# A four-layer graph network on one core: first pass by slots with four x buffers, halved adjacency loads, later weight loads, shorter batch norms, one more layer norm by slots, and a reordered last step

## What is computed

```python
x = LN(x + L0(x, adj))  # A_hat x; W1, batch norm, relu; W2, batch norm
x = LN(x + L1(x, adj))  # edge softmax attention over 256 edges, 4 heads
x = LN(x + L2(x, adj))  # (adj*adj) mixes before W1 (128->256), W2 (256->512), W3 (512->128)
x = LN(x + L3(x, adj))  # dense masked attention
```

## Time and profile before

| | |
|---|---|
| three runs | 565.99, 568.5, 569.31 us; median 568.5 |
| the profiled execution's own time | 569.67 us |
| its span, first to last instruction | 567.8 us |
| granted TensorE clock, mean | 0.987 of full speed |
| TensorE matmul busy | 533.0 us, 94% of the span |
| VectorE, ScalarE, GpSimd busy | 419.2, 373.9, 198.8 us |

### The profile page before, as it was taken

How to read it: one execution, slowest core, us unless ns; L and a number is a source line. 1 busy time by engine, 2 the same in 40 slices (tenths; PEclk the granted TensorE clock), 3 DMA queues, 4 the chain that set the end, 5 groups by cost and what they waited for, 6 DMA issues and landing times.

```text
span 567.8 us, 11229 instructions
## 1 busy us (share of the span) xinstructions
PE 533.0 (94%) x3522; PEld 464.6 (82%) x3522; DVE 419.2 (74%) x1466; ACT 373.9 (66%) x749; POOL 198.8 (35%) x240
## 2 busy tenths in 40 slices
PE   7899999797999989999999999999999999999871
PEld 5788734575887988998999999999998998989861
DVE  4588677889787644479787787788688776778887
ACT  4577594676656636256695785786787687685681
POOL 7930350337366312315226126216216116210203
PEclk9899999999999999999999999999999999999997
DMA  8222100132100000000000100100100100100012
GB/s 227 76 81 74 39 0 0 55 95 64 48 0 2 1 0 1 1 2 1 1 2 2 37 1 0 38 0 0 37 0 0 37 0 0 39 0 2 1 38 74
DMA packets 28383, 15.26 MB, mean 27 GB/s; under 512 B 2320, under 2 KB 28048, under 8 KB 28352
## 3 DMA queue, kind: packets, MB, share of 16 engines
q1 hardware_dynamic: 27792, 13.65, 8.4%
q0 software_dynamic: 560, 1.25, 0.7%
HBM read 10.69 MB, written 4.19 MB: 26 GB/s over the span
## 4 chain that ended last, share of the span: by engine, by line
PE 76%; DVE 13%; ACT 3%; issue 2%; POOL 2%; DMA 1%; SPq 1%; DVEq 0%; POOLq 0%; ACTq 0%
PE psum L291 14%; PE psum L293 14%; PE psum L292 14%; PE psum L2004 9%; PE psum L1811 5%; PE psum L1859 3%; PE psum L1946 3%; PE psum L1956 3%; PE psum L1883 2%; PE psum L1870 2%; PE psum L1874 2%; PE psum L2050 2%; PE psum L2032 2%; DVE ln_st L188 2%; DVE soft L1029 1%
## 5 line engine op out<-in xcount | busy, mean ns | idle before, releaser
L207 POOL TENSOR_TENSOR ln_r<-ln_v,mhalf 128x8 f32<-128x8 f32 x27 | 44.6, 1651 | 225.7 <-DVE ln_v L201 225.7
L2004 PE MATMUL psum<-l2w_s,h 128*128 128x128 f32 x512 | 59.8, 276 | 0.0
L2004 PEld LDWEIGHTS psum<-l2w_s,h 128*128 128x128 f32 x512 | 59.0, 192 | 0.8
L291 PE MATMUL psum<-qt_hi,l2w_s_hi 128*128 128x512 f32 x128 | 52.8, 412 | 0.0
L293 PE MATMUL psum<-qt_hi,l2w_s_lo 128*128 128x512 f32 x128 | 50.8, 396 | 0.0
L292 PE MATMUL psum<-qt_lo,l2w_s_hi 128*128 128x512 f32 x128 | 50.7, 396 | 0.0
L285 ACT ACTIVATE keep_x<-keep_x,ln_b,ln_r (+1 forms) x108 | 44.4, 487 | 8.2 <-DVE keep_x L277 5.6
L1559 ACT ACTIVATE h<-psum 128x512 f32<-128x512 f32 x60 | 34.8, 593 | 11.7 <-PE psum L293 11.6
L291 PE MATMUL psum<-wgt_hi,h_hi 128*128 128x256 f32 x128 | 37.1, 290 | 0.9 <-DVE h_lo L1006 0.9
L293 PE MATMUL psum<-wgt_hi,h_lo 128*128 128x256 f32 x128 | 35.8, 280 | 0.0
L292 PE MATMUL psum<-wgt_lo,h_hi 128*128 128x256 f32 x128 | 35.8, 279 | 0.0
(11 more groups left out here) (284 smaller groups left out, 1746.8 us busy)
## 6 DMA issues: line engine op xcount, KB each, us to landing
xin<-in_x SPq DMA_DIRECT2D x64, 128.0 KB, 2.3
out_x<-ob SPq DMA_DIRECT2D x24, 128.0 KB, 1.8
out_x<-keep_x SPq DMA_DIRECT2D x8, 128.0 KB, 1.9
l2w_raw<-in_l2w POOLq DMA_DIRECT2D x1, 512.0 KB, 5.8
adjs<-in_adj SPq DMA_DIRECT2D x1, 256.0 KB, 2.8
adjs<-in_adj_t SPq DMA_DIRECT2D x1, 256.0 KB, 3.0
l2w_s<-in_l2w POOLq DMA_DIRECT2D x1, 256.0 KB, 5.5
w_raw<-in_w_t SPq DMA_DIRECT2D x1, 128.0 KB, 3.0
```

Source lines behind the costliest of these rows:

```text
L207: pool.tensor_tensor(ln.r[:].rearrange("p s k -> p (s k)"), ln.v[:].rearrange("p s k -> p (s k)"), mhalf[:], ALU.pow).then_inc(ln.root, 1)
L291: pe.matmul(o, lhs[0], rhs[0], start=start, stop=False)
L2004: i = pe.matmul(bank(s)[:, 0, k * D:(k + 1) * D], h2[:, s, g, j * N + t * P:j * N + (t + 1) * P], l2w3_s[:, g, :], start=(g == 0), stop=(g ...
```

## The change

The diff, cut to its core. What is left out of it declares semaphores and one tile (`off_diag`, ones with a zero diagonal, made on GpSimd by a fill and two selects of 128 x 256), renumbers waits, and adds in the last step: `end_norm_stats(n)` for n of 2 and 3 (the sums of pair 6, statistics from their slots), `end_power` and `sixth_shift` on GpSimd for the same, `fifth_stats` and `fifth_moments` (pair 5's statistics by slots), and `end_exps(s, j)` by halves. On VectorE x0_low, agg_low, h_stats and on ScalarE x0_high, agg_high, h_raw now take one slot each; `last_stats` reads the hidden values from PSUM. For slot 0 the aggregate is made in two banks, and copied and subtracted by halves.

```diff
 def _(sp):
-    sp.dma_start(adj_sb, adj.rearrange("(t p) m -> p t m", p=P)).then_inc(s_adj, 16)
-    sp.dma_start(adjt_sb, adj_t.rearrange("(t p) m -> p t m", p=P)).then_inc(s_adj, 16)
...
-    sp.dma_start(w1_raw[:], w1_t).then_inc(s_small, 16)
+    for t in range(T):
+        sp.dma_start(adj_sb[:, t, :], adj[t * P:(t + 1) * P, :]).then_inc(s_adj[t], 16)
+    def first_load(q, k):
+        for t in range(T):
+            sp.dma_start(xn[:, 4 + k, t, :, :], x_nat[:, t, bass.ds(2 * q, 2), :]).then_inc(x_in[k], 16)
...
+    for k in range(2):
+        first_load(k, k)
+    sp.dma_start(w1_raw[:], w1_t).then_inc(s_first, 16)
+    for k in range(2, 4):
+        first_load(k, k)
+    for k, v in enumerate((src, dst)):
+        sp.dma_start(edge_i[:, k, :], v.partition_broadcast(P)).then_inc(s_edge, 16)
+    sp.dma_start(ecol_i[:].rearrange("p a t -> p (a t)"), edge_cols).then_inc(s_edge, 16)
     sp.dma_start(w2t[:], w2_t.rearrange("(k p) o -> p k o", p=P)).then_inc(s_small, 16)
     sp.dma_start(bnp[:], bn_cols).then_inc(s_small, 16)
     sp.dma_start(l3a_s[:], l3a).then_inc(s_small, 16)
-    for k, v in enumerate((src, dst)):
...
+        for k in range(4):
+            sp.wait_ge(x0_lo, 4 * g + k - 3)
+            first_load(4 * g + k, k)
+    sp.wait_ge(x0_lo, Q)
...
-            sp.wait_ge(x0_lo, 2 * p + s - 1)
...
     i.then_inc(keys_compared, 1)
+    for to, frm in ((wvq[:, 0, :], wv_t), (wvq[:, 1, :], wq_t), (wot[:], wo_t),
+                    (l2w1_raw[:], l2w1), (l2w2_raw[:], l2w2.rearrange("(k p) g -> p k g", p=P)),
+                    (l2w3_s[:], l2w3.rearrange("(k p) g -> p k g", p=P)), (l3w_s[:], l3w), (l3wt_s[:], l3w_t)):
+        pool.dma_start(to, frm).then_inc(s_wts, 16)
     pool.wait_ge(ranks_ready, 1)
...
-    for q in range(4):
-        if q >= 2:
+    for q in range(6):
+        if 2 <= q < 4:
             pool.wait_ge(ln0_done[1], q - 1)
         first_power(pool, q, ln0, q < 2)
-    ln_power(pool, 2, ln0)
-    with pool.Fori(2, IT - 1) as p:
+    for s in range(2):
+        split_x1(2, s, False)
+    ln_power(pool, 3, ln0)
+    with pool.Fori(3, IT - 1) as p:
...
-    dve.tensor_tensor(degc[:, 2, :], degc[:, 0, :], degc[:, 1, :], ALU.subtract).then_inc(deg_ready, 1)
-    dve.wait_ge(at_ready, 1)
+    dve.wait_ge(at_ready, T)
+    dve.tensor_tensor(degc[:, 2, :], degc[:, 0, :], degc[:, 1, :], ALU.add).then_inc(deg_ready, 1)
...
-    link(dve.tensor_copy(a_hat[0][:], at1[:]))
-    dve.tensor_tensor(a_hat[1][:], at1[:], a_hat[0][:], ALU.subtract).then_inc(a_hat_ready, 1)
...
+        dve.scalar_tensor_tensor(out=at1[:, t, :], in0=at1[:, t, :], scalar=dinv[:, t:t + 1],
+                                 in1=bank(0)[:, 0, 0:N], op0=ALU.mult, op1=ALU.mult).then_inc(at_scaled, 1)
+    for t in range(T):
+        dve.wait_ge(a_hat_hi, t + 1)
+        dve.tensor_tensor(a_hat[1][:, t, :], at1[:, t, :], a_hat[0][:, t, :], ALU.subtract).then_inc(a_hat_ready, 1)
+    x0_low(1, 1)
...
+    for s in range(2):
+        agg_low(s, s)
+        x0_low(2 + s, 2 + s)
+    def pass1(p, k):
+        for s in range(2):
+            agg_low(2 * p + s, s)
+            x0_low(2 * p + 2 + s, k + s)
+            h_stats(2 * p - 2 + s)
+    pass1(1, 0)
...
     dve.wait_ge(keys_compared, 1)
     dve.tensor_reduce(rank[:], less[:], AX_X, ALU.add).then_inc(ranks_ready, 1)
-    x0_low(1)
-    with dve.Fori(1, IT - 1) as p:
-        agg_low(p)
-        x0_low(p + 1)
-        h_stats(p - 1)
-    agg_low(IT - 1)
-    h_stats(IT - 2)
-    h_stats(IT - 1)
+    pass1(2, 2)
+    with dve.Fori(1, (IT - 2) // 2) as g:
+        for i in range(2):
+            pass1(2 * g + i + 1, 2 * i)
+    agg_low(Q - 2, 0)
+    h_stats(Q - 4)
+    dve.wait_ge(h_out, Q - 2)
+    dve.bn_stats(bst1[:, 0, Q - 3, :], hraw[:, 0, Q - 3, :])
+    agg_low(Q - 1, 1)
+    dve.bn_stats(bst1[:, 1, Q - 3, :], hraw[:, 1, Q - 3, :]).then_inc(h_stat, 1)
+    for s in range(2):
+        last_stats(Q - 2 + s, s)
     dve.wait_ge(h_stat, Q)
...
-        bn_link(dve.tensor_tensor(shift, shift, scale, ALU.mult))
-        return dve.tensor_tensor(shift, shift, beta, ALU.add)
+        for n, k in enumerate(range(ks.start, ks.stop)):
+            i = dve.scalar_tensor_tensor(out=bco[:, 3, k:k + 1], in0=bco[:, 2, k:k + 1], scalar=bco[:, 0, k:k + 1],
+                                         in1=beta[:, n:n + 1], op0=ALU.mult, op1=ALU.add)
+        return i
...
+    dve.wait_ge(bn2_ready, 1)
+    dve.tensor_scalar(bnt[:, 0, N:2 * N], oraw[:, 0, N:2 * N], bco[:, 2, 2:3], bco[:, 3, 2:3], ALU.mult, ALU.add).then_inc(bnt_half, 1)
...
     first_apply(dve, 3, ln0, range(4), ln0_done[1], 2)
     sum0_slot(2, 0)
+    first_stats(dve, 4, ln0)
     x1_low(3)
+    first_moments(dve, 4, ln0, False)
     sum0_slot(2, 1)
     leaky_slot(0, 1)
-    variance0(2, False)
-    sum0(3)
-    apply0(2)
-    body(1, False)
-    with dve.Fori(2, IT - 3) as p:
+    first_stats(dve, 5, ln0)
+    first_apply(dve, 4, ln0, range(4), ln0_done[0], 2)
+    first_moments(dve, 5, ln0, False)
+    sum0_slot(3, 0)
+    first_apply(dve, 5, ln0, range(4), ln0_done[1], 2)
+    sum0_slot(3, 1)
+    leaky_slot(1, 0)
+    variance0(3, False)
+    leaky_slot(1, 1)
+    sum0(4)
+    apply0(3)
+    body(2, False)
+    with dve.Fori(3, IT - 3) as p:
         body(p)
...
     leaky3(M, 0)
-    s3_low(L, 0)
+    fifth_stats(0)
     leaky3(M, 1)
     slot_sum3(K, 1)
-    ln_stats(dve, last_sum, K, ln3)
+    s3_low(L, 0)
+    fifth_stats(1)
+    fifth_moments()
     ln_var_eps(dve, K, ln3)
     add(L, 0, o2_done, 2, ln2)
     end_norm_stats(0)
     weights3(M, False)
     end_norm(0)
+    s3_low(L, 1)
     dve.wait_ge(exr_done, 2 * M + 2)
     slot_scores(L, 0, 1, s12_ok)
-    s3_low(L, 1)
     slot_scores(L, 0, 0, own_ok)
-    end_maxima(0)
     add(L, 1, o2_done, 3, ln2)
     end_norm_stats(1)
+    end_maxima(0)
+    end_norm(1)
+    dve.wait_ge(exr_done, 2 * M + 4)
+    slot_scores(L, 1, 1, s12_ok)
     end_highest(0)
     end_leaky(0)
-    end_norm(1)
-    dve.wait_ge(exr_done, 2 * M + 4)
-    slot_scores(L, 1, 1, s12_ok)
     slot_scores(L, 1, 0, own_ok)
     end_maxima(1)
     end_highest(1)
...
-    ln_stats(dve, row(M), M, ln3)
-    ln_var_eps(dve, M, ln3)
+        end_norm_stats(2 + s)
...
+    for t in range(T):
+        act.dma_start(adjt_sb[:, t, :], adj_t[t * P:(t + 1) * P, :]).then_inc(s_adj[t], 16)
+    act.preload_act_table_set("sqrt_and_others")
+    for t in range(T):
+        act.wait_ge(s_adj[t], 32)
+        act.activation(at1[:, t, :], adjt_sb[:, t, :], ACT.Copy, accum_out=degc[:, 0, t:t + 1]).then_inc(at_ready, 1)
...
+    x0_high(0, 0)
+    for t in range(T):
+        act.wait_ge(at_scaled, t + 1)
+        act.activation(a_hat[0][:, t, :], at1[:, t, :], ACT.Copy).then_inc(a_hat_hi, 1)
+    x0_high(0, 1)
+    for s in range(2):
+        agg_high(s, s)
+        x0_high(0, 2 + s)
...
+    def pass1(p, g, k):
+        for s in range(2):
+            h_raw(2 * p - 2 + s, s)
+            agg_high(2 * p + s, s)
+            x0_high(g, k + s)
+    for i in range(2):
+        pass1(1 + i, 1, 2 * i)
+    with act.Fori(1, (IT - 2) // 2) as g:
+        for i in range(2):
+            pass1(2 * g + i + 1, g + 1, 2 * i)
+    for s in range(2):
+        h_raw(Q - 4 + s, s)
+        agg_high(Q - 2 + s, s)
...
+    def relu0(q, frm):
+        for k in range(H0 // P):
+            act.activation(hraw[:, k, q, :], frm(k), ACT.Relu, bias=bco[:, 3, k:k + 1],
+                           scale=bco[:, 2, k:k + 1]).then_inc(relu_ready, 1)
+    for q in range(3):
+        relu0(q, lambda k: hraw[:, k, q, :])
     act.wait_ge(edges_sorted, 1)
     act.activation(sorted_bc[:], bank(6)[:, 0, :].rearrange("p (a e) -> p a e", a=2), ACT.Copy)
+    act.activation(sorted_col[:], bank(7)[:, 0, 0:ET], ACT.Copy).then_inc(sorted_out, 1)
+    with act.Fori(3, Q - 2) as q:
+        relu0(q, lambda k: hraw[:, k, q, :])
+    for s in range(2):
+        relu0(Q - 2 + s, lambda k: bank(2 + 2 * s + k)[:, 0, :])
...
+    act.activation(bnt[:, 0, 0:N], oraw[:, 0, 0:N], ACT.Identity, bias=bco[:, 3, 2:3], scale=bco[:, 2, 2:3]).then_inc(bnt_ready, 1)
+    bn_out_slot(0, 1, True)
+    for s in range(2):
+        bn_out_slot(1, s, False)
...
     for s in range(2):
         bn_out_slot(3, s, False)
         gathered_slot(1, s)
-    scale0(2)
-    for s in range(2):
+    for s in range(2):
+        bn_out_slot(4, s, False)
         projected(1, s)
-    for s in range(2):
-        bn_out_slot(4, s, False)
     edge_log()
     scale0(3)
...
     relu1(2, 1)
     attended(K, 0)
     relu1(3, 2)
-    for s in range(2):
-        slot_sums(M, s)
+    slot_sums(M, 0)
+    attended(K, 1)
+    slot_sums(M, 1)
+    exps(M, 0)
     s3_high(L, 0)
-    attended(K, 1)
     relu1(0, 3)
-    exps(M, 0)
     relu1(1, 4)
     exps(M, 1)
+    ln_scale(act, last_sum, K, 0, ln3)
     s3_high(L, 1)
     for u, base in ((0, 6), (1, 4)):
         for j in range(2):
             end_copied(u, j, base)
+    ln_scale(act, last_sum, K, 1, ln3)
+    for j in range(2):
```

(83 more changed lines are left out.)

251 lines of the change are left out of this document (125 added, 126 removed).

## The result

| | before | changed |
|---|---|---|
| median of the undisturbed runs, us | 568.9 (565.99 to 571.63) | 560.4 (560.28 to 562.57) |
| ratio, 95% interval | | 0.987 (0.9825 to 0.9914) |
| profiled execution, us | 569.67 | 560.28 |
| its span, us | 567.8 | 558.5 |
| its mean granted clock | 0.987 | 0.983 |

What follows compares the result with a forecast made beforehand. TensorE was taken as the bound, with losses at the ends and joints and VectorE in the tail. Gains of 2.1 + 6.0 + 0.8 + 0.6 + 0 + 3.3 = 12.8 gave 555.7 us from the median 568.5, range 550.5 to 561.0.

Steps and rivals of the forecast that it cites:

- lies under the landing: nothing: Head: the new diagonal mask, two more selects on POOL, was to cost nothing under the landing of the loads.
- the 0.5 for the table load: Head: moving ScalarE's table load of 1.28 ahead of its wait, hidden under the landing, was to gain 0.5 us.
- the 1.6 for loads and halving: Head: halved adjacency loads and copies by halves, letting TensorE begin on half of A_hat, were to gain 1.6 us.
- the head gains nothing: Rival, head: the loads are not earlier, so 2.1 less gain, 557.8 us; chance 0.04.
- The split: Pass 1: of 6.9 us over pure work, 2.4 idle and 1.5 lower clock from the comparison, 2.2 from TensorE's order.
- VectorE binds pass 1 while POOL works: Rival, pass 1: VectorE, slowed beside POOL, limits the gain to 3 instead of 6, 558.7 us; chance 0.12.
- VectorE shows no idle time in 18 to 40: Sign, pass 1: VectorE without idle time in 18 to 40 us would show the prediction wrong.
- I put 0: Layer 1's start: the third norm by slots was to change nothing in sum, bounds -3 and +3.
- the rival with 0.14: Rival, layer 1's start: TensorE idles 4 in one piece and the clock drops, costing 3, 558.7 us; chance 0.14.
- My third sign: Layer 1's start: the granted clock falling for longer than before would show the prediction wrong.
- Slower: Rival, pass 1: VectorE's slot exceeds TensorE's 2.83 throughout; gains gone from 3.73, near 572 us at 4.0; chance 0.03.
- a tail that only swaps waits: Rival, tail: the reordering only swaps waits, 559.0 us; chance 0.08.

Runs made afterwards that it cites:

- mask_last: The changed kernel with the new diagonal mask made last of POOL's constants; first real matmul at 8.54 instead of 9.22, time 561.6 us, no ratio.
- key_late: The kernel before, with VectorE waiting for the key comparison one round of pass 1 later; time 567.1 us, no ratio.
- old_orders: The changed kernel with pass 1 ordered by pairs again on TensorE, VectorE and ScalarE, keeping four x buffers and the later comparison; 566.5 us, no ratio.
- turn5_both: The changed kernel, ScalarE making turn five's blocks before scaling slot 7 and copying the third pair's projections before scaling slot 9; 556.5 us, ratio 0.979.
- ramp_old: The changed kernel with layer 1's third norm as a pair again on VectorE, ScalarE and POOL; 558.4 us, ratio 0.980.
- old_tail: The changed kernel with the last step put back as before on TensorE, VectorE, ScalarE and POOL; 563.5 us, ratio 0.992.
- best_slots: The changed kernel with turn5_both's ScalarE order, the mask made last, and VectorE's third-pair leaky step ahead of scaling slot 8; 554.0 us, ratio 0.976.
- ramp_spin: The changed kernel with six warming matmuls on TensorE between the third gather and turn five; 559.4 us, no ratio.
- ramp_old_again: The same kernel as ramp_old, against the kernel before, measured a second time in five rounds; 558.7 us, ratio 0.983.
- best_pairs: The changed kernel with layer 1's third norm as a pair (as ramp_old) and the mask made last; 557.7 us, ratio 0.982.

## Why the prediction was right or wrong

Two steps failed, one in the head and one in layer 1's start, and together they make the missing 3.5 of 12.8 (1.2 and 2.6, less 0.3 that other parts gave over their terms).

**The head: wrong in size.** 0.9 came for 2.1. The first step that failed is the sentence on the new diagonal mask, that it "lies under the landing: nothing". It lies under the landing for VectorE, but TensorE waited for the same counter, and its warming matmuls slid by 1.24 onto the moment at which dinv comes. I had costed the operation and not the wait behind it. mask_last gives 0.7 of it back. The other 0.5 is in the 0.5 for the table load and the 1.6 for loads and halving, which no run separates: the two together made the degrees ready 1.07 sooner (dinv at 5.70 instead of 6.77) and, with the mask last, the way from dinv to the first matmul 0.7 shorter (2.73 instead of 3.39). The rival "the head gains nothing" did not come, although the landing it rests on was indeed no earlier.

**Pass 1: right sum, wrong parts.** 46.0 were forecast and 46.0 came, with the clock at 1.00, which is luck in part, since two wrong parts make up the sum. The split (3.9 from the comparison and its clock, 2.2 from the order) is wrong: key_late gives 1.8, and old_orders against the changed kernel 4.3 for the order. I had taken the waits of a quiet stretch, 0.3 a pair, for what the order saves, and not asked what becomes of POOL's contention in 24 to 40 once the comparison no longer hides it. My rival "VectorE binds pass 1 while POOL works" is what the old order does. My sign that "VectorE shows no idle time in 18 to 40" very nearly came (21.42 busy of 22.00 in the changed kernel), and yet TensorE was busy for all 22.00: as a sign of a loss it was no good. The key comparison's reduction came at 21.40 and not at "about 18", which cost nothing, as POOL was issuing the weight loads until 22.38.

**The joint, the second norm:** 1.0 for 0.8 and 0.4 for 0.6. The half block took ScalarE 0.60 (128x256 at 93.03), not half of the 0.80 of a whole one.

**Layer 1's start: the rival came true.** "I put 0" was wrong by 2.6, inside the bound of 3, and in the way that the rival with 0.14 describes (idle in one piece, then the clock). My walk down the queues put turn five 0.9 later and found the fourth gather 0.5 sooner "at full clock"; that assumption is the second step that failed. Turn five itself was only 0.3 late (8.14 sooner than before, where turn one was 8.43 sooner), but from there to the gather it took 11.26 us at a clock of 0.56, where turn5_both took 6.08 at 1.00. The walk without the clock may have been sound: with 6.08 the gather would be at 133.4 (an estimate, 127.28 + 6.08), and ramp_old, the old order at full clock, has it at 134.13. My third sign, a lower clock in layer 1's start for longer than before, came. And the slowing beside POOL that the walk counted on for slot 5's norm (2.43 instead of 1.12) did come: 2.34, at 116.25. The rival deserved the larger chance, since the trace of before already had a clock of 0.75 behind waits of 0.95 to 1.43.

**The tail:** 3.5 for 3.3, and old_tail (3.4) confirms it from the other side.

**Slower, a tail that only swaps waits, a head that gains nothing:** none of these came. What brought the time to the edge of the range was that two terms, the head and layer 1, both missed on the same side; a range made of single losses has little room for two.

Still open: why the clock falls behind turn five in the changed kernel's order every time, though filling the hole did not prevent it, and why it falls in some executions of the same instructions and not in others. No kernel here can tell, since none controls it.

## What to carry to other kernels

When a queue written by hand has its engine waiting for a late input, look at what stands behind that wait and is ready; moving ready work ahead of it (turn5_both, best_slots) won 4 to 6 us over the changed kernel, where the slot-wise norm that had created the wait had won nothing. A semaphore that counts many producers hands every one's delay to every waiter: cost an added step for each engine that waits on its counter. And compare kernels at equal granted clock before believing a difference of a few us: here one stretch at the lower level is worth from 1.7 (6.97 against 5.30) to about 5 (11.26 against 6.08).

## What was unexpected about the hardware

The clock fell without TensorE having stood still. In turn5_both it was busy for 29.99 of 30 us from 150 to 180, and the clock fell to 0.53 at 169, right behind 16 matmuls of 4 output columns, which in three other places of that trace it did not. It had stayed at 1.00 from 130.5 to 143.7, where TensorE was busy for only 10.46 of 13.20. And in ramp_spin, where the hole was filled with 256-column matmuls, it fell anyway once the scores came. The Trainium skill (TensorE: Matmul & The Clock Gate, HAM oscillation) explains the lower level by gaps without matmuls; these two traces show it with hardly a gap, and the measurement decides: here the absence of gaps was no protection.

The same instructions behind nearly the same waits (ramp_old, ramp_old_again, key_late, best_pairs, before) took 5.30, 5.30, 5.30, 6.97 and 6.97 us from the scores to the fourth gather. In these five profiles it is two values, not a scatter.
